# One of sixteen C products per tile, moved from VectorE to GpSimd, in a Mamba and mixture-of-experts kernel

## The chip, the cores and the metric

The kernel runs on one core of a Trainium2 chip. The metric is the device time of one execution, in microseconds (us). Below, PE is TensorE, DVE is VectorE, ACT is ScalarE, POOL is GpSimd and SP is SyncE, as in the profile; "span" is the stretch that the profiler covers, and times in timelines count from its start.

## What is computed

The reference is a selective state space layer and then a mixture of experts, on 4 sequences of 1024 tokens with 256 features. The change touches only the scan of the first layer and its product with C:

```python
deltaA  = jnp.exp(delta[..., None] * A)                 # (b, l, 512, 16)
deltaBx = (delta * xs)[..., None] * B[:, :, None, :]
_, ys = jax.lax.associative_scan(combine, (deltaA, deltaBx), axis=1)   # h = deltaA * h + deltaBx
y = jnp.einsum('blcn,bln->blc', ys, C)                  # sum over the 16 states
out = (y + xs * D) * res
return x + out @ w_out
```

All of it is float32. There are 512 channels and 16 states, so 8192 recurrences of 1024 steps for each sequence.

## The kernel before

**Tiles and steps.** The 4096 tokens are cut into 8 tiles (k = 0 to 7) of 512 tokens; a sequence is two tiles. A tile has 16 steps (q = 0 to 15, `NQ`), numbered Q = 16k + q over the run. A step handles 4 x 512 recurrence elements on each of 128 partitions, in four parts r = 0 to 3 (`NR`). The 16 steps are 4 channel chunks c of 4 steps f. After the eight tiles an expert stage follows, which the change does not touch.

**One step on the engines.**

- POOL, `input_step` (L474): one instruction of 128x2048 makes u times B into buffer `X[:, Q % 4]`; there are four buffers (`NX = 4`). It waits until the sum of step Q - 4 has been taken from that buffer (`y_acc`), and at the first step of a chunk until the replicated operand `rep` has arrived from memory.
- ACT, `decay` (L970): four exponentials of 128x512 into the four PSUM parts `psH[:, r]`. Each waits until the product of the step before has left that part (`hc_ready`). In even tiles `keep_state` (L959) first copies the last column of the part into `carry`, for the tile that continues the sequence.
- DVE, `scan` (L1135): four scans in place in `psH`, and `output_step` (L1144): four products `X = psH * C4`, each issued one scan later than the scan it reads. Step 9's last product is thus issued behind step 10's first scan.
- PE, `add_state` (L1492): four matmuls with `gsum` add the products to `psY`. They raise `y_acc` by one, which is what POOL waits for to reuse the buffer.

**The order of the rest.** All queues are written out by hand. PE's order for a tile is `PE_STEPS`: at step n it does the work `first`, then `add_state(Q - 1)`, then the work `rest`. Around the change these are:

```python
9:  ([("D", 0, 1)], [("D", 1, 1), ("R", 0, -1), ("R", 1, -1)]),
10: ([], [("L", 0, -1), ("U", 0, -1)]),
11: ([("U", 1, -1)], [("I", 4, 1)]),
12: ([("U", 2, -1)], [("N", 0, -1)]),
```

D is the projection of the next tile's time step (L1412), R the transposes of the previous tile's rows (L1419), L the router (L1429), U one part of the shared expert's first matrix (`up`, L1457), I the input projection (L1383), N the shared expert's second matrix (`down`, L1473). The router waits for ACT's two copies of the transposed rows (`read_nT`, recorded at the helper's line L800).

POOL's order after `input_step(k, q)`: at q = 4 and 6 `input_chunk(k, 2)` and `(k, 3)`, at q = 13 and 14 `input_chunk(k + 1, 0)` and `(k + 1, 1)` (four instructions of 128x512 each, L456 to L462, that make the operands which SP then stores and loads back as `rep`); at q = 3 `place`, at q = 4, 5, 6, 8 two scatters each, at q = 7 `roots`, at q = 15 `choose` (small instructions of the router of the tile before). SP loads the `rep` of the next tile's chunk 0 after `input_chunk(k + 1, 0)`, and that of chunk 1 (used from step 4) behind `load_c(k + 1, 3)`, which waits for step 15's last product.

Of the kernel before, what the change touches and what calls it, by code (L numbers as in the profile page):

```python
# [16 lines left out]
ALU = mybir.AluOpType  # L17
# [7 lines left out]
P = 128  # L25
TC = 512
# [21 lines left out]
def build(nc, x, norm_scale, w_in, conv_w, conv_b, A_log, D_skip, w_xproj, w_dt, b_dt, w_out,  # L48
# [4 lines left out]
    HALVES = L // TC  # L53
# [12 lines left out]
    NR = 4  # L66
    GJ = P // NR
    NF = N * GJ // P
    NG = N // NF
    NQ = CH * NF  # L70
# [38 lines left out]
    with ExitStack() as whole:  # L109
        def sem(name):  # L110
            return whole.enter_context(nc.semaphore(name))
# [52 lines left out]
        psH = whole.enter_context(nc.psum_tensor("psH", [P, NR, TC], F32))  # L164
# [11 lines left out]
        NX = 4  # L176
        X = big[:, half:].rearrange("p (n r t) -> p n r t", n=NX, r=NR)
# [34 lines left out]
        C4 = sb("C4", [P, NF, TC])  # L212
# [61 lines left out]
        scan_done = sem("scan_done")  # L274
        carry_done = sem("carry_done")
        hc_ready = sem("hc_ready")
        y_acc = sem("y_acc")
        z_done = sem("z_done")

# [111 lines left out]
                eng.wait_ge(p_free[bank_of(k, use)], PLACE[k, use] // 2 + 1)  # L391


        def products(Q, r):

            return Q * NR + r + 1

        def summed(Q):

# [28 lines left out]
        def _(pool):  # L428
# [35 lines left out]
            def input_step(k, q):  # L464

                c, f = q // NF, q % NF
                g, Q = k * CH + c, k * NQ + q
                if f == 0:
                    pool.wait_ge(rep_here[g % 2], 64 * (g // 2 + 1))
                if c == 0:  # L470
                    pool.wait_ge(b_here[f], 64 * (k + 1))
                if Q >= NX:
                    pool.wait_ge(y_acc, summed(Q - NX))
                nc.gpsimd.tensor_tensor(X[:, Q % NX], rep[:, g % 2, 1],  # L474
                                        B4[:, f:f + 1, :].broadcast_to([P, NR, TC]),
                                        ALU.mult).then_inc(bx_ready, 1)

            link = Chain(pool, p_link)

            def roots(k):  # L480
# [67 lines left out]
            for k in range(NT):  # L548
                for q in range(NQ):
                    input_step(k, q)  # L550
                    if q in (4, 6):
                        input_chunk(k, q // 2)
                    if k >= 2 and q == 3:
                        place(k - 2)
                    if k >= 2 and q in SCATTER_AT:
                        scatter(k - 2, SCATTER_AT[q])
                    if k >= 1 and q == 7:
                        roots(k - 1)
                    if k >= 1 and q == 15:
                        choose(k - 1)  # L560
                    if q in (13, 14) and k + 1 < NT:
                        input_chunk(k + 1, q - 13)
# [223 lines left out]
        def _(act):  # L786
# [168 lines left out]
            def keep_state(Q, r):  # L955
                k, q = Q // NQ, Q % NQ
                if Q >= 0 and k % HALVES == 0:
                    last = psH[:, r, TC - 1:TC]
                    nc.scalar.activation(carry[:, q, r:r + 1], last, ACT.Copy).then_inc(carry_done, 1)  # L959
                    act.wait_ge(carry_done, (k // HALVES) * NQ * NR + q * NR + r + 1)  # L960

# [123 lines left out]
        def _(dve):  # L1085
# [41 lines left out]
            def scan(k, q, r):  # L1127
                Q = k * NQ + q
                if r == 0:
                    dve.wait_ge(bx_ready, Q + 1)  # L1130
                    if k % HALVES:
                        dve.wait_ge(carry_done, (k // HALVES) * NQ * NR + (q + 1) * NR)
                dve.wait_ge(dA_ready, Q * NR + r + 1)
                start = carry[:, q, r:r + 1] if k % HALVES else 0.0
                nc.vector.tensor_tensor_scan(psH[:, r, :], psH[:, r, :], X[:, Q % NX, r, :], start,  # L1135
                                             ALU.mult, ALU.add).then_inc(scan_done, 1)

            def output_step(Q, r):

                f = Q % NF  # L1140
                if Q % NQ < NF:
                    dve.wait_ge(c_here[f], 64 * (Q // NQ + 1))
                dve.wait_ge(scan_done, Q * NR + r + 1)
                nc.vector.tensor_tensor(X[:, Q % NX, r, :], psH[:, r, :], C4[:, f, :],  # L1144
                                        ALU.mult).then_inc(hc_ready, 1)

# [211 lines left out]
        def _(pe):  # L1358
# [127 lines left out]
            def add_state(Q):  # L1486
                g, f = Q // NF, Q % NF
                if f == 0:
                    skip(g // CH, g % CH)
                for r in range(NR):  # L1490
                    pe.wait_ge(hc_ready, products(Q, r))
                    ins = nc.tensor.matmul(psY[r * GJ:(r + 1) * GJ, :], gsum[:], X[:, Q % NX, r, :],  # L1492
                                           start=False, stop=(f == NF - 1), skip_group_check=True)
                ins.then_inc(y_acc, 1)
# [26 lines left out]
            for k in range(NT + 2):  # L1521
                for n in range(NQ):
                    first, rest = pe_step(k, n)
                    Q = k * NQ + n
                    work(first)
                    if k < NT or (k == NT and n == 0):
                        if Q:
                            add_state(Q - 1)
                    work(rest)

# [80 lines left out]
```

## Time and profile before

| | |
|---|---|
| time, median of 3 runs | 1692.61 us (1691.77 to 1694.22) |
| the profiled execution: its own time | 1698.09 us |
| the profiled execution: span | 1696.1 us |
| scan stage (the eight tiles) | about 65 to 1055 us of the span |
| DVE busy over the span | 70% (in slices of the scan stage nine tenths or more) |
| POOL busy over the span | 56% |
| PE busy over the span | 87%, mean granted clock 0.925 |

Busy shares are averages over two stages with different limits. A row of a timeline gives start, duration, engine, line and operation, the shapes written and read, how many instructions are merged in it (x8), and in brackets the idle time before it with the engine that ended it. A matmul in float32 is recorded as two, so the four matmuls of `add_state` are x8.

### The profile page before, as it was taken

The page shows a single profiled execution, that of the slowest core. Times are in us where ns is not written, and L with a number is a line of the kernel's source. Part 1 is how long each engine was busy: PE and PEld are TensorE (multiplying, and loading weights), DVE is VectorE, ACT ScalarE, POOL GpSimd, SP SyncE. Part 2 cuts the span into 40 slices and gives each one's busy share as a digit, 9 for nine tenths or more (in the row PEclk, how much of TensorE's full clock was granted, in tenths as well). Part 3 has the DMA queues.
Part 4 walks back from the last instruction along what each step waited for, and adds up shares of the span by engine and source line. Part 5 has one row for each costly group of instructions (what it writes and reads, how often), then busy time and mean ns, then how long its engine had stood idle before and what let it go on. Part 6 is the DMA issues. An engine that isn't in the chain of part 4 may idle for free.

```text
span 1696.1 us, 24636 instructions
## 1 busy us (share of the span) xinstructions
PE 1474.3 (87%) x6945; PEld 958.2 (56%) x6946; DVE 1192.2 (70%) x2113; ACT 907.8 (54%) x1778; POOL 951.7 (56%) x590
## 2 busy tenths in 40 slices
PE   7386888999989989889989779989999999999970
PEld 3121324535535535436435335779999999999960
DVE  4489999999999999999999999213333333333327
ACT  4477667777766777766877543223233333323324
POOL 1586796898898898898898884301111111111115
PEclk9599997997998999998989789899999999999995
DMA  5833743663554545635635531745555555555538
GB/s 157 222 87 85 165 103 85 143 149 87 146 130 122 129 112 136 137 97 131 137 97 123 145 79 35 260 169 190 193 185 185 191 194 190 194 195 189 185 125 263
DMA packets 137447, 252.14 MB, mean 149 GB/s; under 512 B 15809, under 2 KB 68914, under 8 KB 137250
## 3 DMA queue, kind: packets, MB, share of 16 engines
q1 hardware_dynamic: 130898, 233.49, 49.8%
q0 software_dynamic: 6480, 17.83, 2.9%
q8 instruction: 30, 0.49, 0.1%
q14 instruction: 39, 0.32, 0.1%
HBM read 205.76 MB, written 45.51 MB: 148 GB/s over the span
## 4 chain that ended last, share of the span: by engine, by line
PE 45%; DVE 39%; issue 7%; ACT 6%; DMA 1%; SPq 1%; POOL 0%; DVEq 0%; ACTq 0%; POOLq 0%
DVE psH L1135 26%; PE psH L1553 15%; PE psP L1564 14%; DVE big L1144 8%; PE psP L1394 4%; PE psA L1492 2%; PE psA L1473 2%; PE psP L1457 2%; PE psP L1383 1%; PE psP L1503 1%; ACT psH L970 1%; PE psP L1541 1%; DVE res L1152 1%; ACT xs L846 1%; DVE st6f L1337 1%
## 5 line engine op out<-in xcount | busy, mean ns | idle before, releaser
L474 POOL TENSOR_TENSOR big<-big,B 128x2048 f32<-128x2048 f32 x128 | 578.2, 4531 | 103.1 <-PE psA L1492 46.2
L970 ACT ACTIVATE psH<-big,A_q 128x512 f32<-128x512 f32 x512 | 352.4, 691 | 155.1 <-DVE big L1144 129.3
L1144 DVE TENSOR_TENSOR big<-psH,C 128x512 f32<-128x512 f32 x512 | 345.3, 675 | 0.0
L1135 DVE TENSOR_TENSOR_SCAN psH<-psH,big 128x512 f32<-128x512 f32 x256 | 312.0, 1219 | 41.1 <-POOL big L474 20.9
L578 POOL DMA_INDIRECT con_dram<-eo,dest x71 | 68.1, 959 | 471.4 <-ACT eo L1043 463.5
L1135 DVE TENSOR_TENSOR_SCAN psH<-psH,carry,big 128x512 f32<-128x512 f32 x256 | 327.4, 1279 | 7.2 <-ACT psH L970 7.2
L1553 PEld LDWEIGHTS psH<-nTb,ew_s 128*128 128x128 f32 x2272 | 266.1, 193 | 4.2 <-issue 0.7
L1553 PE MATMUL psH<-nTb,ew_s 128*128 128x128 f32 x2272 | 266.5, 276 | 0.3 <-issue 0.3
L1564 PE MATMUL psP<-big,hT 128*128 x1136 | 257.0, 379 | 0.7 <-DVE eb L1302 0.7
L1492 PE MATMUL psA<-big,gsum 128*32 128x512 f32 x1024 | 224.1, 659 | 30.5 <-DVE big L1144 30.2
L1564 PEld LDWEIGHTS psP<-big,hT 128*128 128x128 f32 x1136 | 210.3, 190 | 26.8 <-issue 1.1
L1273 DVE TENSOR_TENSOR hT<-psH,vecs 128x512 f32<-128x512 f32 x142 | 98.2, 692 | 178.3 <-PE psH L1553 178.3
L1039 ACT ACTIVATE hT<-hT 128x512 f32<-128x512 f32 x142 | 89.4, 630 | 193.3 <-DVE hT L1273 192.2
L1383 PE MATMUL psP<-xnT,w_in_s 128*128 128x512 f32 x256 | 131.4, 639 | 29.8 <-ACT spr L800 26.8
L1457 PE MATMUL psP<-nT,sw_s 128*128 128x256 f32 x512 | 140.5, 427 | 0.5 <-ACT xs L800 0.5
L1457 PEld LDWEIGHTS psP<-nT,sw_s 128*128 128x128 f32 x512 | 108.2, 216 | 41.0 <-issue 18.2
L1394 PE MATMUL psP<-xraw,convd 128*128 128x512 f32 x256 | 120.2, 613 | 12.2 <-ACT xs L800 8.6
L1302 DVE TENSOR_TENSOR eb<-psP,eb_s 128x256 f32<-128x256 f32 x71 | 30.2, 425 | 141.0 <-PE psP L1564 141.0
L1492 PEld LDWEIGHTS psA<-big,gsum 128*32 128x32 f32 x1024 | 33.5, 111 | 167.5 <-DVE big L1144 117.0
L1473 PE MATMUL psA<-sw_s,hT 128*128 128x256 f32 x512 | 126.7, 395 | 0.0
L1043 ACT ACTIVATE eo<-eb,wt 128x256 f32<-128x256 f32 x71 | 36.1, 509 | 163.0 <-DVE eb L1302 163.0
L1473 PEld LDWEIGHTS psA<-sw_s,hT 128*128 128x128 f32 x512 | 98.0, 196 | 43.3 <-issue 30.6
(174 smaller groups left out, 1532.9 us busy)
## 6 DMA issues: line engine op xcount, KB each, us to landing
ew_s<-in_L_ffn_ew_dram SPq DMA_DIRECT2D x71, 1024.0 KB, 4.9
big<-ud_dram SPq DMA_DIRECT2D x128, 512.0 KB
ud_dram<-ud SPq DMA_DIRECT2D x32, 512.0 KB
xb<-rows_dram SPq DMA_DIRECT2D x71, 130.0 KB, 2.1
B<-bc_dram SPq DMA_DIRECT2D x128, 64.0 KB, 5.1
C<-bc_dram SPq DMA_DIRECT2D x128, 64.0 KB, 4.7
big<-in_L_ffn_ew_dram SPq DMA_DIRECT2D x8, 1024.0 KB
big<-con_dram SPq DMA_DIRECT2D x16, 512.0 KB, 8.8
```

Of the source, the lines that this page charges most:

```text
L474: nc.gpsimd.tensor_tensor(X[:, Q % NX], rep[:, g % 2, 1], B4[:, f:f + 1, :].broadcast_to([P, NR, TC]), ALU.mult).then_inc(bx_ready, 1)
L970: nc.scalar.activation(psH[:, r, :], rep[:, g % 2, 0, r, :], ACT.Exp, scale=A_q[:, c, r, f:f + 1]).then_inc(dA_ready, 1)
L1135: nc.vector.tensor_tensor_scan(psH[:, r, :], psH[:, r, :], X[:, Q % NX, r, :], start, ALU.mult, ALU.add).then_inc(scan_done, 1)
L1144: nc.vector.tensor_tensor(X[:, Q % NX, r, :], psH[:, r, :], C4[:, f, :], ALU.mult).then_inc(hc_ready, 1)
L1273: nc.vector.tensor_tensor(hT[:, par, a * (HC // 2):(a + 1) * (HC // 2), :], psH[:, 2 * par + a, :].rearrange("p (c t) -> p c t", t=P), bia ...
L1383: ins = nc.tensor.matmul(dst, w_in_s[:, d, m * P:(m + 1) * P], xnT[:, d, :], start=(d == 0), stop=(d == DC - 1))
L1394: ins = nc.tensor.matmul(dst, convd[:, j * CH + c, :], xraw[:, c % 2, j:j + TC], start=(j == 0), stop=(j == K - 1))
L1457: ins = nc.tensor.matmul(dst[:, j * 2 * P:(j + 1) * 2 * P], sw1_s[:, d, m * P:(m + 1) * P], nT[:, d, h * 2 * P:(h + 1) * 2 * P], start=(d ...
L1473: ins = nc.tensor.matmul(psS[:, t * O:(t + 1) * O], hT2[:, i % 2, j, t * P:(t + 1) * P], sw2_s[:, 2 * p + j, :], start=False, stop=(p == P ...
L1492: ins = nc.tensor.matmul(psY[r * GJ:(r + 1) * GJ, :], gsum[:], X[:, Q % NX, r, :], start=False, stop=(f == NF - 1), skip_group_check=True)
L1553: ins = nc.tensor.matmul(psH[:, 2 * par + a, j * P:(j + 1) * P], ew1_s[:, par, d, m * P:(m + 1) * P], nTb[:, par, d, :], start=(d == 0), s ...
L1564: ins = nc.tensor.matmul(psP[:, 1, 0:O], hT[:, par, m, :], ew2_s[:, e, m, :], start=(m == 0), stop=(m == HC - 1))
```

## The change

In step 9 of each tile (`QP = 9`, the tenth) DVE's four scans write into the buffer `X` instead of `psH` and raise `hc_ready` themselves; DVE makes no product for that step. POOL makes the product over the whole buffer in one instruction of 128x2048, in place. POOL does it after `input_step(k, 11)`, and waits for the four scans, for C, and in even tiles for ACT's four copies of the last column (which now read `X`). PE adds step 9 only when POOL's product is there (`by_pool`), and does so later in its order: not between R and L of step 10, but at n = 11 behind `first` (U1), just ahead of the sum of step 10.

```diff
+        QP = 9
+
         def products(Q, r):
 
-            return Q * NR + r + 1
+            swapped = {(QP - 1, NR - 1): 1, (QP, 0): -1}
+            return Q * NR + r + 1 + swapped.get((Q % NQ, r), 0)
+
+        def scanned(Q, r):
+
+            return Q * NR + r + 1 - NR * ((Q + NQ - 1 - QP) // NQ)
...
+            def output_step(k, q):
+
+                f, Q = q % NF, k * NQ + q
+                pool.wait_ge(hc_ready, products(Q, NR - 1))
+                pool.wait_ge(c_here[f], 64 * (k + 1))
+                if k % HALVES == 0:
+                    pool.wait_ge(carry_done, (k // HALVES) * NQ * NR + (q + 1) * NR)
+                nc.gpsimd.tensor_tensor(X[:, Q % NX], X[:, Q % NX], C4[:, f:f + 1, :].broadcast_to([P, NR, TC]),
+                                        ALU.mult).then_inc(by_pool, 1)
...
                     input_step(k, q)
+                    if q == QP + 2:
+                        output_step(k, QP)
...
-                    last = psH[:, r, TC - 1:TC]
+                    last = (X[:, Q % NX, r] if q == QP else psH[:, r])[:, TC - 1:TC]
...
-                nc.vector.tensor_tensor_scan(psH[:, r, :], psH[:, r, :], X[:, Q % NX, r, :], start,
-                                             ALU.mult, ALU.add).then_inc(scan_done, 1)
+                to = X[:, Q % NX, r, :] if q == QP else psH[:, r, :]
+                nc.vector.tensor_tensor_scan(to, psH[:, r, :], X[:, Q % NX, r, :], start,
+                                             ALU.mult, ALU.add).then_inc(hc_ready if q == QP else scan_done, 1)
...
+                if Q % NQ == QP:
+                    return
...
-                    pe.wait_ge(hc_ready, products(Q, r))
+                    if Q % NQ == QP:
+                        pe.wait_ge(by_pool, Q // NQ + 1)
+                    else:
+                        pe.wait_ge(hc_ready, products(Q, r))
...
-                        if Q:
+                        if Q and n != QP + 1:
+                            if n == QP + 2:
+                                add_state(Q - 2)
                             add_state(Q - 1)
```

## Rows read from the trace of the kernel before

**Rows 1.** The page, busy time of each engine over the span

```profile
PE 1474.3 (87%) x6945; PEld 958.2 (56%) x6946; DVE 1192.2 (70%) x2113; ACT 907.8 (54%) x1778; POOL 951.7 (56%) x590
```

**Rows 2.** The page, the costliest group of instructions by line

```profile
L474 POOL TENSOR_TENSOR big<-big,B 128x2048 f32<-128x2048 f32 x128 | 578.2, 4531 | 103.1 <-PE psA L1492 46.2
```

**Rows 3.** Timeline of VectorE, part of step 6, k = 4 (start, us, engine, line)

```profile
606.52 1.22 DVE L1135 TENSOR_TENSOR_SCAN psH<-psH,big 128x512 f32<-128x512 f32 x1
607.65 0.67 DVE L1144 TENSOR_TENSOR big<-psH,C 128x512 f32<-128x512 f32 x1
608.24 1.22 DVE L1135 TENSOR_TENSOR_SCAN psH<-psH,big 128x512 f32<-128x512 f32 x1
```

**Rows 4.** Timeline of GpSimd, k = 3, step 9 to the next tile's step 0

```profile
498.88 13.45 POOL L474 TENSOR_TENSOR big<-big,B 128x2048 f32<-128x2048 f32 x3
...
514.48 9.17 POOL L474 TENSOR_TENSOR big<-big,B 128x2048 f32<-128x2048 f32 x2 [2.15 <-PE psA L1492]
527.34 1.27 POOL L456 TENSOR_TENSOR spe<-spe,ud 128x512 f32<-128x512 f32 x1 [3.68 <-ACT ud L883]
...
532.51 4.53 POOL L474 TENSOR_TENSOR big<-big,B 128x2048 f32<-128x2048 f32 x1
...
542.17 4.54 POOL L474 TENSOR_TENSOR big<-big,B 128x2048 f32<-128x2048 f32 x1
...
549.87 4.54 POOL L474 TENSOR_TENSOR big<-big,B 128x2048 f32<-128x2048 f32 x1
```

**Rows 5.** Timeline of VectorE, k = 3, last scan of step 9

```profile
513.25 1.29 DVE L1135 TENSOR_TENSOR_SCAN psH<-psH,carry,big 128x512 f32<-128x512 f32 x1
```

**Rows 6.** Timeline of TensorE, k = 3, steps 9 to 11, and of ScalarE

```profile
517.40 1.63 PE L1492 MATMUL psA<-big,gsum 128*32 128x512 f32 x8
519.29 3.56 PE L1429 MATMUL psP<-rwT,nT 128*128 128x8 f32 x16 [0.25 <-ACT nT L800]
522.69 6.32 PE L1457 MATMUL psP<-nT,sw_s 128*128 128x256 f32 x16
528.95 1.06 PE L1492 MATMUL psA<-big,gsum 128*32 128x512 f32 x8
...
518.45 0.69 ACT L800 ACTIVATE nT<-psP,vecs 128x512 f32<-128x512 f32 x1
```

**Rows 7.** Timeline of TensorE, sum of step 10, k = 1, 4, 6; router, k = 4

```profile
283.18 1.06 PE L1492 MATMUL psA<-big,gsum 128*32 128x512 f32 x8
...
642.25 1.92 PE L1429 MATMUL psP<-rwT,nT 128*128 128x8 f32 x16 [0.76 <-ACT nT L800]
...
649.34 1.06 PE L1492 MATMUL psA<-big,gsum 128*32 128x512 f32 x8
...
898.03 1.07 PE L1492 MATMUL psA<-big,gsum 128*32 128x512 f32 x8
```

**Rows 8.** Timeline of VectorE, the first scan after k = 1, 3, 4, 6

```profile
313.11 1.22 DVE L1135 TENSOR_TENSOR_SCAN psH<-psH,big 128x512 f32<-128x512 f32 x1
...
559.68 1.22 DVE L1135 TENSOR_TENSOR_SCAN psH<-psH,big 128x512 f32<-128x512 f32 x1
...
681.41 1.28 DVE L1135 TENSOR_TENSOR_SCAN psH<-psH,carry,big 128x512 f32<-128x512 f32 x1
...
927.41 1.28 DVE L1135 TENSOR_TENSOR_SCAN psH<-psH,carry,big 128x512 f32<-128x512 f32 x1
```

**Rows 9.** Timeline of GpSimd, end of k = 0 and start of k = 1

```profile
164.80 4.51 POOL L474 TENSOR_TENSOR big<-big,B 128x2048 f32<-128x2048 f32 x1
...
179.82 9.01 POOL L474 TENSOR_TENSOR big<-big,B 128x2048 f32<-128x2048 f32 x2 [0.88 <-DMA big<-ud_dram]
```

**Rows 10.** Timeline of GpSimd, step 4 and step 8 in k = 4

```profile
576.16 4.54 POOL L474 TENSOR_TENSOR big<-big,B 128x2048 f32<-128x2048 f32 x1 [6.86 <-DMA big<-ud_dram]
...
615.58 4.52 POOL L474 TENSOR_TENSOR big<-big,B 128x2048 f32<-128x2048 f32 x1
```

**Rows 11.** Timeline of VectorE, k = 4, first scan of step 8

```profile
620.25 1.22 DVE L1135 TENSOR_TENSOR_SCAN psH<-psH,big 128x512 f32<-128x512 f32 x1
```

More of the change, by code:

```diff
@@ L276, in build @@
         hc_ready = sem("hc_ready")
+        by_pool = sem("by_pool")
         y_acc = sem("y_acc")
@@ L1134, in scan @@
                 start = carry[:, q, r:r + 1] if k % HALVES else 0.0
-                nc.vector.tensor_tensor_scan(psH[:, r, :], psH[:, r, :], X[:, Q % NX, r, :], start,
-                                             ALU.mult, ALU.add).then_inc(scan_done, 1)
+                to = X[:, Q % NX, r, :] if q == QP else psH[:, r, :]
+                nc.vector.tensor_tensor_scan(to, psH[:, r, :], X[:, Q % NX, r, :], start,
+                                             ALU.mult, ALU.add).then_inc(hc_ready if q == QP else scan_done, 1)
             def output_step(Q, r):
                 f = Q % NF
-                if Q % NQ < NF:
+                if Q % NQ == QP:
+                    return
+                if Q % NQ < NF or Q % NQ == QP + NF:
                     dve.wait_ge(c_here[f], 64 * (Q // NQ + 1))
-                dve.wait_ge(scan_done, Q * NR + r + 1)
+                dve.wait_ge(scan_done, scanned(Q, r))
                 nc.vector.tensor_tensor(X[:, Q % NX, r, :], psH[:, r, :], C4[:, f, :],
```

## The prediction, made before the changed kernel was run

> **What bounds the kernel now.** I first read the busy times on the page [rows 1]: PE is busiest over the span, but the change lies in the scan stage, where the slices of the page show DVE at nine tenths or more. So I went on to the timelines of that stage. They show a pair of scan and product on DVE starting every 1.72 us (606.52 to 608.24), the product taking 0.59 us of that: 607.65 to 608.24 [rows 3]. Four pairs are 6.9 us a step. Is DVE alone the bound? The second view is POOL's group for the products with B [rows 2]: 578.2 us in 128 instructions of 4.53 us, with 103.1 us idle ahead of them, most of it ended by PE's `add_state`. POOL is therefore held by buffers coming free as well as by its own work. In step 8 of tile 4 POOL's input ends at 615.58 + 4.52 = 620.10 [rows 10] and DVE's scan starts at 620.25 [rows 11]: there POOL has no lead at all. It has built up since step 4, whose input waits 6.86 us for the loaded `rep` [rows 10]. That load is released by the end of the previous tile's last product, so DVE's and POOL's ways through steps 0 to 8 both start at DVE's step 0. A delay or gain of that step passes on whole to the next tile. What counts is then how much earlier or later DVE can start step 0 of the next tile.
>
> **What DVE saves.** Four products leave step 9: 4 x 0.59 = 2.36 us a tile. The scans keep their shape, and only write elsewhere. A scan into SBUF has no row here; I take the 1.22 us of [rows 3], and would not expect the write alone to cost more than a few hundredths. A scan behind a scan has no row either. From below its distance is 1.13 us (606.52 to 607.65), which I take, since the parts are independent; from above it is the full 1.22 us, which would cost 4 x 0.09 = 0.36 us a tile. If nothing else held DVE, eight tiles would save 18.9 us.
>
> **What POOL's product costs.** It has the shape of the product with B: 4.53 us [rows 2]. In tile 3 POOL is through with the inputs of steps 9 to 11 at 498.88 + 13.45 = 512.33 [rows 4]. The last scan of step 9 ends at 513.25 + 1.29 = 514.54 [rows 5], less three removed products, 1.77, that stood ahead of it: 512.8. So POOL waits 0.5 us, makes the product to 517.3 and the input of step 12 to 521.9. DVE wants that input two steps after 512.8, at 526.6 or later, so nothing is late yet.
>
> The Trainium skill, "GPSIMD Engine Reference", section 4.1, speaks against such a move: elementwise work with two inputs belongs on VectorE, because GpSimd is about twice as slow. The rows say 4.53 against 2.36 us, so the trace agrees; by that rule alone 2.2 us of engine time would be lost a tile. Neither figure enters the sum, since the product fits into idle time.
>
> **What is late next.** The input of step 13 goes into the buffer of step 9, so it waits for `add_state` of step 9. Before, that sum ran at 517.40 to 519.03, in front of the router, which started at 519.29 behind ACT's copy (518.45 + 0.69 = 519.14) [rows 6]. It lay in time in which PE had to wait for ACT anyway. Now it is queued behind the router (3.56 us), U0 and U1 (6.32 us). The router can't start sooner, since ACT's copy ends when it did: it hangs on the D and R work before it. U1 therefore ends where the sum of step 10 started, at 528.95, and the sum of step 9 runs in its place, 1.06 us at the rate of that row, to 530.0 [rows 6]. POOL starts the input of step 13 some 0.15 us later (the input of step 12 started at 514.48), at 530.2. It has stood idle since 521.9.
>
> What is queued behind it on POOL: that input (4.53), the chunk for the next tile, the input of step 14, the other chunk, the input of step 15, `choose`, and the next tile's input 0. From the start of the chunk to the end of that input 0 the trace has 527.34 to 549.87 + 4.54 = 554.41, that is 27.07 us with no wait between [rows 4]. So the next tile's input 0 is ready 4.53 + 27.07 = 31.6 us after the input of step 13 starts, at 561.8. DVE's step 0 started at 559.68 [rows 8]. The result for tile 3: +2.1 us, where DVE by itself would have come 2.36 us early.
>
> **The same for the other tiles.** Ready = (end of step 10's sum) + 0.15 + 31.6, against DVE's old start. k = 1: 284.24 gives 316.0 against 313.11, +2.9. k = 4: 650.40 gives 682.15 against 681.41, +0.7. k = 6: 899.10 gives 930.85 against 927.41, +3.4 [rows 7, 8]. These are the first, the earliest and the last of the six tiles 1 to 6; tile 2 read the same way gives +3.5 and tile 5 +2.1. In even tiles POOL also waits for ACT's four copies. Each must come ahead of step 10's exponential of its part, so they are there when DVE is through with step 10 at the latest, and the 8 us of idle time before input 13 hold that too. Tile 0 has no shared-expert work on PE at this place and POOL has a lead, so it keeps -2.36; tile 7 prepares no next tile, -2.36.
>
> A second way leads over ACT: I4, U2 and N0 on PE come up to 1.06 us later, and with them ACT's reads and the exponentials queued behind them in step 13. That is under POOL's delay in all of the six but tile 4 (+0.7), where it could add 0.3 us at most. I leave it out.
>
> The sum: 2.9 + 3.5 + 2.1 + 0.7 + 2.1 + 3.4 - 2 x 2.36 = +10.0 us. The profiled execution took 1698.09 us by its own time, 2 us over its span, and would take 1708.1. It lies 5.5 us over the median of the runs shown, so for that median I predict 1692.6 + 10.0 = 1702.6 us.
>
> **The clock.** The same router took 3.56 us in tile 3 and 1.92 us in tile 4 [rows 6, 7]; the granted clock stood at half (1.2 GHz) in the one and at full (2.4 GHz) in the other. With step 9's sum gone from in front of the router, PE idles 1.6 us more there. If tile 4's router then falls to half clock too, its input 13 starts 1.64 us later. If the sum itself ran at the 1.63 us of [rows 6] instead of 1.06, six tiles would lose 3.4 us. I leave both out of the sum and in the range. From the other side, if the router ran at full clock in the five other tiles, the release would come 1.64 us sooner in each, 8.2 us in all: +1.8.
>
> The Trainium skill, "TensorE: Matmul & The Clock Gate", section "HAM oscillation — how this bites in real kernels", says that gaps in which PE is idle make the gate halve its clock. By that rule the wider gap ahead of the router can only cost; no row yet shows this gap.
>
> **The rivals.**
>
> - *The saving comes through (faster).* The place is the end of the chain above. If POOL's input 0 were ready by DVE's old start less 2.36 us, each tile would gain 2.36: 1692.6 - 18.9 = 1673.7 us. For that the input of step 13 would have to start 4.5 us sooner in tile 3, before 525.8. Then U1 would have to end 4.4 us sooner than 528.95, and PE's router and U0 and U1 (9.9 us together) would have to run at full clock throughout. Against it: only tile 4 comes near. Parts of it, with a net gain over 0.2%, are included: 0.11.
> - *No change.* The router's full clock of the paragraph above gives +1.8, 1694.4 us; likewise if half of the queue before U1 moved forward with DVE's earlier step 10. Against it: ACT's copy ends the router's wait, and it does not hang on step 9's products: 0.13.
> - *The loads come late (slower still).* The `rep` of the next tile's chunk 0 is stored and loaded after the first chunk. At the end of tile 0 the chunk ended at 164.80 and the load let POOL go at 179.82, 15.0 us later [rows 9]. In the chain above 17.4 us lie between (31.6 - 4.53 less the chunk's 5.17 and input 0's 4.54), so the load is hidden with 2.4 us to spare. If it takes 4.4 us longer, each of six tiles loses another 2 us: 1714.6. Chance 0.08.
> - *The forecast*, slower with POOL late: 0.68, with 1697 to 1709 us as its own range (the clock's 1.64 + 3.4 upward, half of its 8.2 and some more downward).
>
> The 0.2% that a measurement of this kernel can tell from no change is 3.4 us. The chances are then faster 0.11, same 0.13, slower 0.76. The range of 8 in 10 takes in the forecast and most of the case of no change: 1693 to 1710 us.
>
> **What would show it.** In the profile after: in step 9 DVE scans 1.1 to 1.2 us apart with no product; POOL's new line at 4.53 us, started within a microsecond or so of the last scan in odd tiles; then POOL idle some 8 us ahead of the input of step 13 in tile 3, ended by PE's `add_state`; that `add_state` directly behind U1; DVE waiting for POOL at step 15 and at step 0 of the next tile, in tiles 1 to 6. If POOL is idle there but DVE doesn't wait for it, my 31.6 us are wrong. If the sum of step 9 ends well before the old start of step 10's sum, PE's order is not the bound that I take it for, and the time comes out lower.

## The result: 0.9% slower, and the profile after

The changed kernel takes 1708.03 us (median of 4 runs, 1707.47 to 1708.63), the kernel before 1692.19 us beside it (1690.75 to 1694.22). The ratio is 1.0093, with a 95% interval of 1.0075 to 1.011: slower by 15.8 us. The profiled execution took 1707.71 us by its own time, with a span of 1705.9 us and a mean granted clock of 0.911. The page's busy times, and its chain of what ended last:

```profile
PE 1479.9 (87%) x6945; PEld 962.8 (56%) x6946; DVE 1175.7 (69%) x2081; ACT 905.8 (53%) x1778; POOL 987.1 (58%) x598
...
PE 45%; DVE 23%; POOL 15%; issue 8%; ACT 6%; DMA 1%; SPq 1%; DVEq 0%; POOLq 0%; ACTq 0%
```

Against [rows 1] DVE has 32 instructions and 16.5 us less, POOL 8 instructions and 35.4 us more. So the work moved as the diff says. In the chain POOL has 15%; in the chain of the kernel before it had 0%, and DVE 39%. The chain now runs over POOL. Its timeline in tile 3, to be held against [rows 4]:

```profile
502.38 13.48 POOL L482 TENSOR_TENSOR big<-big,B 128x2048 f32<-128x2048 f32 x3
517.67 4.52 POOL L493 TENSOR_TENSOR big<-big,C 128x2048 f32<-128x2048 f32 x1 [1.81 <-DVE big L1156]
522.15 4.53 POOL L482 TENSOR_TENSOR big<-big,B 128x2048 f32<-128x2048 f32 x1
534.37 4.55 POOL L482 TENSOR_TENSOR big<-big,B 128x2048 f32<-128x2048 f32 x1 [7.68 <-PE psA L1518]
...
561.39 13.49 POOL L482 TENSOR_TENSOR big<-big,B 128x2048 f32<-128x2048 f32 x3
```

L493 is the new product; L482 is the old L474, and L1518 the old `add_state`. The row at 534.37 is the input of step 13, the one at 561.39 begins with the next tile's input 0. POOL stands idle for 7.68 us before input 13, until PE has taken the sum of step 9. From there to input 0 POOL has no more waits. Why the sum comes late is in PE's timeline of the same place, beside [rows 6]:

```profile
521.08 0.66 PE L1442 MATMUL psP<-ident,xrow 128*128 128x128 f32 x4 [0.83 <-ACT spr L820]
523.54 3.55 PE L1452 MATMUL psP<-rwT,nT 128*128 128x8 f32 x16 [1.81 <-ACT nT L820]
526.95 6.32 PE L1480 MATMUL psP<-nT,sw_s 128*128 128x256 f32 x16
533.19 1.92 PE L1518 MATMUL psA<-big,gsum 128*32 128x512 f32 x16
```

The router (L1452) now starts 1.81 us after the transposes; U0 and U1 (L1480) follow, and the two sums (x16) come last. Who pays is DVE, at step 15 of this tile (558.26) and at step 0 of the next (565.94):

```profile
558.26 1.29 DVE L1156 TENSOR_TENSOR_SCAN psH<-psH,carry,big 128x512 f32<-128x512 f32 x1 [1.45 <-POOL big L482]
...
565.94 1.23 DVE L1156 TENSOR_TENSOR_SCAN psH<-psH,big 128x512 f32<-128x512 f32 x1 [0.48 <-POOL big L482]
```

**Where the time went.** The length of a tile is read here from its first scan (as in [rows 8]) to the next tile's, for tile 7 to the end of its last scan. In us, tiles 0 to 7:

| | 0 | 1 | 2 | 3 | 4 | 5 | 6 | 7 |
|---|---|---|---|---|---|---|---|---|
| before | 121.8 | 122.4 | 122.6 | 124.0 | 121.7 | 124.0 | 122.0 | 124.6 |
| after | 121.0 | 123.9 | 126.1 | 126.3 | 126.6 | 126.0 | 126.0 | 118.6 |
| after less before | -0.8 | +1.5 | +3.5 | +2.3 | +4.9 | +2.0 | +4.0 | -6.0 |
| predicted | -2.4 | +2.9 | +3.5 | +2.1 | +0.7 | +2.1 | +3.4 | -2.4 |

The eight add up to +11.4 us, against +9.8 for the spans. The one large miss on the losing side is tile 4. In the kernel before, its router and U ran at a granted clock of 0.76, in the changed kernel at 0.57 (columns: us, PE, PEld, DVE, ACT and POOL busy, PEclk, DMA share, GB/s). First the kernel before, from the router's start to U1's end in tile 4 and in tile 3:

```profile
642.20:649.40 7.20, 7.15 (x36) 6.02 (x40) 7.20 (x9) 7.07 (x15) 3.89 (x1) 0.76 0.19 67
519.20:529.00 9.80, 9.71 (x36) 8.29 (x40) 9.80 (x12) 7.95 (x13) 6.12 (x3) 0.55 0.14 40
```

The same two stretches of the changed kernel:

```profile
650.30:659.80 9.50, 9.48 (x36) 8.10 (x40) 8.78 (x15) 8.18 (x17) 7.74 (x2) 0.57 0.04 14
523.50:533.20 9.70, 9.66 (x34) 8.23 (x34) 9.65 (x17) 7.71 (x13) 3.19 (x1) 0.55 0.11 27
```

Tile 4's stretch grew from 7.2 to 9.5 us. Tile 3's was already long. The other 1.8 us by which tile 4's sum of step 9 came later than reckoned lie ahead of this stretch: the router started 84.4 us into the tile instead of 82.6. TensorE's clock was low there before the wider gap was reached, as the second half of the transposes shows, first in the kernel before, then in the changed one:

```profile
639.38 0.66 PE L1419 MATMUL psP<-ident,xrow 128*128 128x128 f32 x4 [0.82 <-ACT spr L800]
...
647.39 1.12 PE L1442 MATMUL psP<-ident,xrow 128*128 128x128 f32 x4 [0.37 <-ACT spr L820]
```

### The profile page after: what moved, and what is told of

Its sections match the earlier page's. It is cut to its first block, busy times and chain, and to the rows that moved or that the text cites. A ratio compares the mean times of both kernels' runs of the same rounds, so it can differ in the third digit from the quotient of the medians.

```text
span 1705.9 us, 24652 instructions
## 1 busy us (share of the span) xinstructions
PE 1479.9 (87%) x6945; PEld 962.8 (56%) x6946; DVE 1175.7 (69%) x2081; ACT 905.8 (53%) x1778; POOL 987.1 (58%) x598
## 4 chain that ended last, share of the span: by engine, by line
PE 45%; DVE 23%; POOL 15%; issue 8%; ACT 6%; DMA 1%; SPq 1%; DVEq 0%; POOLq 0%; ACTq 0%
PE psH L1581 15%; PE psP L1592 14%; DVE psH L1156 14%; POOL big L482 9%; PE psP L1417 4%; DVE big L1167 4%; PE psA L1518 2%; PE psP L1406 2%; PE psA L1496 2%; PE psP L1480 1%; PE psP L1435 1%; POOL big L493 1%; ACT psH L990 1%; POOL ud L467 1%; POOL ud L470 1%
## 5 line engine op out<-in xcount | busy, mean ns | idle before, releaser
L482 POOL TENSOR_TENSOR big<-big,B 128x2048 f32<-128x2048 f32 x128 | 578.2, 4533 | 65.7 <-PE psA L1518 39.6
L990 ACT ACTIVATE psH<-big,A_q 128x512 f32<-128x512 f32 x512 | 352.0, 690 | 149.6 <-DVE big L1167 125.9
L1156 DVE TENSOR_TENSOR_SCAN psH<-psH,big 128x512 f32<-128x512 f32 x240 | 292.0, 1219 | 61.1 <-POOL big L482 30.8
L1167 DVE TENSOR_TENSOR big<-psH,C 128x512 f32<-128x512 f32 x480 | 322.8, 673 | 0.0
L1156 DVE TENSOR_TENSOR_SCAN psH<-psH,carry,big 128x512 f32<-128x512 f32 x240 | 306.3, 1278 | 19.2 <-ACT psH L990 12.5
L1518 PE MATMUL psA<-big,gsum 128*32 128x512 f32 x1024 | 212.5, 652 | 43.0 <-DVE big L1167 35.0
L1406 PE MATMUL psP<-xnT,w_in_s 128*128 128x512 f32 x256 | 144.0, 692 | 29.3 <-ACT spr L820 26.9
L1480 PE MATMUL psP<-nT,sw_s 128*128 128x256 f32 x512 | 140.0, 426 | 0.5 <-ACT xs L820 0.5
L1518 PEld LDWEIGHTS psA<-big,gsum 128*32 128x32 f32 x1024 | 31.5, 112 | 179.1 <-DVE big L1167 115.6
L1480 PEld LDWEIGHTS psP<-nT,sw_s 128*128 128x128 f32 x512 | 107.5, 215 | 41.0 <-issue 17.7
```

The costliest lines, as they stand in the source:

```text
L482: nc.gpsimd.tensor_tensor(X[:, Q % NX], rep[:, g % 2, 1], B4[:, f:f + 1, :].broadcast_to([P, NR, TC]), ALU.mult).then_inc(bx_ready, 1)
L990: nc.scalar.activation(psH[:, r, :], rep[:, g % 2, 0, r, :], ACT.Exp, scale=A_q[:, c, r, f:f + 1]).then_inc(dA_ready, 1)
L1156: nc.vector.tensor_tensor_scan(to, psH[:, r, :], X[:, Q % NX, r, :], start, ALU.mult, ALU.add).then_inc(hc_ready if q == QP else scan_done, 1)
L1406: ins = nc.tensor.matmul(dst, w_in_s[:, d, m * P:(m + 1) * P], xnT[:, d, :], start=(d == 0), stop=(d == DC - 1))
L1480: ins = nc.tensor.matmul(dst[:, j * 2 * P:(j + 1) * 2 * P], sw1_s[:, d, m * P:(m + 1) * P], nT[:, d, h * 2 * P:(h + 1) * 2 * P], start=(d ...
```

## The experiments

Each is timed in rounds beside the kernel before on the same chip, save `before_again`, which is one profiled execution. The theory is the prediction's: the place of the sum in PE's order holds POOL's buffer. The rivals are POOL's product itself, and the clock.

**The order alone.** On the kernel before: DVE still makes all products.

```diff
-                        if Q:
+                        if Q and n != 10:
+                            if n == 11:
+                                add_state(Q - 2)
                             add_state(Q - 1)
```

> The kernel before with one edit: DVE still makes all products, but PE adds step 9 where the changed kernel does, at n = 11 behind U1 and ahead of the sum of step 10. Theory (the place of the sum in PE's order holds the buffer of step 9 and with it POOL): POOL's input 13 starts at the same moment as in the changed kernel, 94 to 95 us into a tile, and the next tile's step 0 is as late; the product on DVE lies in time in which DVE waits for POOL anyway. So the time is near that of the changed kernel, 1703 to 1710 us. Rival (GpSimd's additional 4.53 us of work a tile is what makes it late): the time stays near the kernel before, 1690 to 1694 us.

Measured: 1712.54 us against 1693.17, ratio 1.0103 (1.0086 to 1.012). POOL in tile 3 of this kernel, inputs 12 and 13:

```profile
521.94 4.53 POOL L474 TENSOR_TENSOR big<-big,B 128x2048 f32<-128x2048 f32 x1 [3.12 <-PE psA L1492]
...
537.68 4.54 POOL L474 TENSOR_TENSOR big<-big,B 128x2048 f32<-128x2048 f32 x1 [11.21 <-PE psA L1492]
```

The whole loss of the changed kernel is there without any product on POOL: it comes from moving one sum behind U1. The time is 2.5 us over the range expected. By tiles this kernel is 1.2, 1.6 and 2.4 us longer than the changed one in tiles 0, 1 and 7 (122.2, 125.5 and 121.0 us) and within 0.4 in the five between; so DVE's saving is seen in tiles 1 and 7, perhaps in tile 0, and nowhere else.

**The sum one place earlier.** On the changed kernel, with the sum of step 9 between U0 and U1:

```diff
+                    if k < NT and n == QP + 2:
+                        add_state(Q - 2)
                     work(first)
...
-                            if n == QP + 2:
-                                add_state(Q - 2)
```

> The changed kernel with PE's sum of step 9 one place earlier, ahead of U1. Theory: the sum ends about 2.5 us sooner in each of tiles 1 to 6 (half of the 6.3 us that U0 and U1 take, less a slower sum), so input 13 and the next tile's step 0 come that much sooner: 1708 - 15 = 1693 us, 1689 to 1698. Rival (GpSimd's added work): POOL's order is untouched, so no change from 1708 us.

Measured: 1689.40 us, ratio 0.9968 (0.9951 to 0.9985). One part of U less in front of the sum turns a loss of 0.9% into a gain of 0.3%. It ends 90.2 to 91.8 us into the tile here, 92.2 to 94.9 in the changed kernel.

**Earlier still.** Between the router and U0:

```diff
-                    work(rest)
+                    if k < NT and n == QP + 1:
+                        work(rest[:1])
+                        add_state(Q - 1)
+                        work(rest[1:])
+                    else:
+                        work(rest)
```

> The changed kernel with PE's sum of step 9 between the router and U0. Theory: the sum ends some 5.5 us sooner than in the changed kernel; POOL's input 0 is then ready before DVE wants it in odd tiles, and about level in even tiles, where POOL's product waits for ACT's copies of the state until 82 to 83 us into the tile. What is left of the 2.36 us a tile on DVE shows: 1675 to 1690 us, 1683 expected, with PE 1.6 us later at U0 and U1. Rival (GpSimd's added work): 1708 us.

Measured: 1692.76 us, ratio 0.9994 (0.9984 to 1.0004). A miss: the sum now ends at 86.1 to 88.4 us, POOL is no longer late, and still nothing is gained over the version with the sum ahead of U1. Against that version DVE's waits for POOL fell over the span from 25.2 us in 9 to 21.1 in 2, and its waits for PE's output projection, which the residual needs, rose from 5.8 us in 2 to 12.0 in 8 (3.19 us of it in tile 7). The waits for ACT's exponentials, 37.8 us in 30, were there already (37.5 in 30; 27.4 in 16 in the kernel before).

**The old place.** In front of the router, on the changed kernel:

```diff
-                        if Q and n != QP + 1:
-                            if n == QP + 2:
-                                add_state(Q - 2)
+                        if Q:
                             add_state(Q - 1)
```

> The changed kernel with PE's sum of step 9 where the kernel before has it, ahead of the router. Theory: in odd tiles GpSimd's product ends at 81 to 82.5 us into the tile, when PE comes to the sum, so the old course is back. In even tiles the product ends at 87 us, and the router and all of PE's work behind it start 3 to 4 us later, which ACT and DVE then wait for. Between the kernel before and the one above: 1680 to 1697 us, 1689 expected. Rival (GpSimd's added work): 1708 us or more.

Measured: 1706.41 us, ratio 1.0073 (1.0056 to 1.0089). A miss, 9 us over the range. PE in tile 4:

```profile
649.39 1.93 PE L1518 MATMUL psA<-big,gsum 128*32 128x512 f32 x8 [5.54 <-POOL big L493]
```

In tiles 2, 4 and 6 PE stands 5.1 to 5.5 us in front of this sum, and the router behind it, since POOL's product isn't there. So the sum can't simply stay where it was; why the product is late follows below.

**The kernel before once more.**

> The kernel before, unchanged, for a second profile. The first profiled execution took 1698.1 us, 5.5 over its median, with 36.2 us for steps 0 to 3 of tile 7 where tiles 3 and 5 took 32.6. If that was a single late stretch, this one lacks it and the span is 1690 to 1694 us; the difference to the changed kernel's span is then near 15 us instead of 9.8.

Measured: a span of 1694.4 us, its own time 1696.42 us, clock 0.933. The tiles took 120.9, 122.4, 121.6, 124.0, 121.7, 124.0, 122.0 and 124.6 us; only tiles 0 and 2 differ from the first profile, by about 1 us each. The guess was wrong: the long stretch in tile 7 is there again, and the span is above the range. But the clock differs in tile 1. Its router and the two parts of U behind it, in the first profile and in this one:

```profile
273.51 3.56 PE L1429 MATMUL psP<-rwT,nT 128*128 128x8 f32 x16 [0.26 <-ACT nT L800]
...
272.06 1.92 PE L1429 MATMUL psP<-rwT,nT 128*128 128x8 f32 x16 [0.46 <-ACT nT L800]
273.84 5.39 PE L1457 MATMUL psP<-nT,sw_s 128*128 128x256 f32 x16
```

The sum of step 10 began 92.5 us into the tile in the one and 88.7 in the other, and the tile took 122.4 us both times. In the kernel before, nothing waits there for that work.

**A quarter of POOL's product.** On the changed kernel:

```diff
-                nc.gpsimd.tensor_tensor(X[:, Q % NX], X[:, Q % NX], C4[:, f:f + 1, :].broadcast_to([P, NR, TC]),
+                nc.gpsimd.tensor_tensor(X[:, Q % NX, 0, :], X[:, Q % NX, 0, :], C4[:, f, :],
```

> The changed kernel with GpSimd's product over one of the four parts of step 9 only (128x512 instead of 128x2048; three parts stay unmultiplied), so some 1.3 us instead of 4.53. Theory (place of the sum): the product lies in time in which GpSimd waits for the sum, so in tiles 1 to 6 nothing moves: 1708 us, 1705 to 1710. Rival (GpSimd's added work counts): 3.3 us less in each of eight tiles, 1682 us.

Measured: 1707.70 us (1707.41 to 1708.86), ratio 1.0078 (1.0061 to 1.0095); the changed kernel has 1708.03. POOL is 25 us less busy (962.1 against 987.1), and no time is gained: the product lies in idle time.

**Step 10 instead of 9.** `QP = 10`, which puts the sum of step 10 behind U2.

> The changed kernel with QP = 10: the eleventh step is treated so instead of the tenth, and everything that hangs on it moves by one step. Theory: now the input of step 14 waits for the late sum, which comes behind U2 at about 99 us into a tile. It stands behind input 13 and a chunk on GpSimd, which end at about the same time, so the next tile's input 0 comes only 2 to 3 us later than in the kernel before, which had 3 to 5 us of lead. The saving on VectorE shows in every tile: 1692 - 8 x 2.36 = 1673 us, 1671 to 1684 with losses where the lead was 3 us. Rival (GpSimd's added work): about 1708 us as for step 9.

Measured: 1705.76 us, ratio 1.0064 (1.0047 to 1.0081). A miss. Tiles 2, 4 and 6 take 125.0, 126.9 and 126.8 us, but tiles 1, 3 and 5 only 121.0, 124.0 and 122.0. POOL in tile 4:

```profile
653.30 4.55 POOL L493 TENSOR_TENSOR big<-big,C 128x2048 f32<-128x2048 f32 x1 [8.57 <-ACT carry L979]
```

and ACT's last copy of the carry there:

```profile
652.94 0.19 ACT L979 ACTIVATE carry<-big 128x1 f32<-128x1 f32 x1
```

In the even tiles 0, 2, 4 and 6 the product waits not for DVE's scans but for four copies of 0.2 us, each of which stands in ACT's order ahead of the next step's exponential of its part. In the changed kernel it is the same wait. POOL's product there, by its line:

```profile
  ACT carry L979: 29.2, 4
  DVE big L1156: 11.0, 3
```

29.2 us in four waits for the copies, 11.0 in three for the scans. In tiles 2, 4 and 6 (5.5 to 5.8 us each) nothing hangs on it, since POOL waits another 2.9 to 3.4 us ahead of input 13. In tile 0 (12.5 us) POOL's queue has no further wait up to input 15, so there the wait counts.

**The copies earlier.** To test that reading: as the last, but in even tiles ACT makes the copies of parts 1 to 3 together, ahead of the second exponential of step 11 (and wait there for the last of step 10's four scans).

```diff
+                early = q == QP + 1 and k % HALVES == 0
...
+                if not early or r == 0:
+                    keep_state(Q - 1, r)
+                elif r == 1:
+                    for other in range(1, NR):
+                        keep_state(Q - 1, other)
```

> The kernel with QP = 10, and in even tiles ScalarE makes its copies of the state of parts 1 to 3 of step 10 one after the other ahead of step 11's second exponential, instead of one ahead of each. In the run without this, GpSimd's product started 5 to 6.5 us after VectorE's last scan of step 10 in even tiles and the next tile's input 0 ended at 125 to 127 us. Theory (the product waits for ScalarE's copies, which stand behind reads of TensorE's results): the product now starts within 1 us of the scan in even tiles too, about 84.5 us into the tile, input 0 ends near 121.5 us, and three even tiles gain 3 to 5 us each: 1706 - 12 = 1694 us, 1689 to 1699. Rival (TensorE's late sum of step 10 sets it): no change from 1706 us.

Measured: 1684.16 us against 1695.36, ratio 0.9938 (0.9919 to 0.9957). The product of tiles 2, 4 and 6 now starts 85.7, 87.6 and 85.1 us into the tile, in the run before 88.9, 90.8 and 90.7. Moving three copies is worth about 1.25%, some 21 us, more than the 7 to 17 expected. 12 of them are in these three tiles (121.8, 123.8 and 121.2 us), 2.2 in tile 0, which is even too. The rest is in the odd tiles; that it comes from POOL being less late there wasn't tested.

**Step 8 instead.** `QP = 8`. The place ahead of the sum of step 9 at n = 10 is in front of the router.

> The changed kernel with QP = 8. Theory: the late sum then stands ahead of step 9's sum and of the router, about 82 us into a tile. Input 12 starts 4 us later than before, input 13 at 86.5, and GpSimd still comes to the next tile's first chunk at 91 to 92 us, when ScalarE has its operands ready as before. So no delay at the tile's end, and VectorE gains; but one of the four removed products lay in a stall for ScalarE's exponentials in step 8, so 1.8 us a tile: 1692 - 14 = 1678 us, 1673 to 1685. Rival (GpSimd's added work): about 1708 us.

Measured: 1679.65 us (1678.39 to 1681.41) against 1695.2, ratio 0.9916 (0.99 to 0.9933). PE in tile 3:

```profile
510.35 2.76 PE L1518 MATMUL psA<-big,gsum 128*32 128x512 f32 x16
513.04 1.95 PE L1452 MATMUL psP<-rwT,nT 128*128 128x8 f32 x16
514.85 3.70 PE L1480 MATMUL psP<-nT,sw_s 128*128 128x256 f32 x16
```

Both sums stand ahead of the router, with no gap before it, and the clock is full from there on:

```profile
513.00:518.50 5.50, 5.50 (x40) 4.77 (x36) 5.50 (x7) 4.62 (x9) 5.50 (x2) 1.00 0.03 12
```

This is the fastest version found. Its six middle tiles take 119.9 to 122.2 us.

**Two steps, 0 and 8.** `QPS = (0, 8)`, the counts of the waits widened to match, the sum of step 0 placed behind what is no U at n = 1, POOL's product of it after input 3.

> Two steps a tile are treated so, 0 and 8; step 0's product follows input 3 on GpSimd, in time in which GpSimd waits for the loaded operand of step 4, and TensorE adds step 0 ahead of the last part of its work at n = 1. If that idle time holds the product and the sum comes before 16.5 us into the tile, VectorE saves 2.36 us more in each tile: 1680 - 19 = 1661 us. In even tiles ScalarE's copies let the product start at 10 to 11 us only and the sum ends near 17, so input 4 comes 1 us late and, with no lead left at step 8, so does that step: 1660 to 1680 us, 1670 expected. If GpSimd's total work has become the bound, 1680 us or more.

Measured: 1684.53 us, ratio 0.9939 (0.992 to 0.9958). A miss: by the ratios it is 0.23% slower than step 8 alone. The two intervals overlap, but its fastest run (1683.66 us) is slower than the slowest of step 8's. Tiles 3 and 5 take 125.6 and 125.9 us. DVE's wait there:

```profile
448.33 0.69 DVE L1189 SCALAR_TENSOR_TENSOR xrow<-xrow,psP 128x512 f32<-128x512 f32 x1 [5.71 <-PE psP L1533]
```

PE waited 2.69 us for the product at n = 1; the output projection behind it came late, and DVE's residual with it (35.0 us in 9 waits, against 3.8 in one with step 8 alone).

**The gap filled.** The runs so far don't separate PE's order from PE's clock. This one keeps the changed kernel's order and adds three matmuls of 128x512 in the gap between R and the router, in tiles 1 to 7. Nothing reads what they write.

```diff
+                    if 1 <= k < NT and n == QP + 1:
+                        pe.wait_ge(rwT_ready, 1)
+                        after(pe, acc_done, 4 * (k - 1))
+                        for i in range(3):
+                            nc.tensor.matmul(psS, skipd[:, 0, :], xs[:, k % 2, 0, :], start=True, stop=True,
+                                             skip_group_check=True)
                     work(rest)
```

> The changed kernel with three extra float32 matmuls (128x512 each, into psS, whose value they destroy for nobody: the next use starts it anew) on TensorE between the transposes R and the router, where the kernel before has the sum of step 9 and the changed one waits 1.8 us for ScalarE. Theory (that gap keeps the granted clock at its lower level through router and U0, U1, which in tile 4 makes the late sum later still): in the even tiles that were partly at full clock before (4 and 6, and by the second profile of before also 2) the late sum ends 2 to 4 us sooner, near 90.7 to 93 us into the tile: 1708 - 8 = 1700 us, 1697 to 1704. Rival (the clock falls for what lies ahead of it, the 3.8 us wait for the projection, and the gap has no part in it): the late sum stays at 94 to 95 us in all six tiles, 1706 to 1710 us.

Measured: 1693.73 us against 1694.33, ratio 0.9995 (0.9981 to 1.0008). That is 14 us faster than the changed kernel, with more work, and below the range expected. PE in tile 3:

```profile
519.59 4.44 PE L1561 MATMUL psA<-xs,skipd 128*128 128x512 f32 x6
523.86 1.85 PE L1452 MATMUL psP<-rwT,nT 128*128 128x8 f32 x16
525.56 3.70 PE L1480 MATMUL psP<-nT,sw_s 128*128 128x256 f32 x16
529.19 1.92 PE L1518 MATMUL psA<-big,gsum 128*32 128x512 f32 x16
```

and the granted clock from the router on, in tiles 4 and 3:

```profile
646.80:652.20 5.40, 5.40 (x34) 4.64 (x32) 4.54 (x6) 4.01 (x9) 5.40 (x2) 1.00 0.00 0
523.80:529.20 5.40, 5.40 (x35) 4.65 (x33) 4.76 (x6) 3.46 (x7) 0.93 (x1) 1.00 0.18 49
```

Router, U0 and U1 take 5.4 instead of 9.7 us, at full clock instead of 0.55. Tiles 1 to 6 take 122.9, 123.7, 124.2, 122.7, 123.0 and 122.7 us: all six are shorter, the odd ones too. (Tile 0, which the edit doesn't touch, took 122.3 against 121.0, so a single tile can move by a microsecond or so.) The extra matmuls don't fit into the pause: in tile 3 the router starts 85.9 us into the tile instead of 83.9. Nor did they keep the clock from falling: while they ran (519.6 to 523.8) the granted clock was 0.59, and from the router on it was full.

**The same matmuls in the kernel before**, as a check that a faster clock isn't worth the same anywhere.

> A control for the run before it: the kernel before, with the same three extra matmuls between the sum of step 9 and the router. If the extra matmuls took 14 us off the changed kernel because its own gap ahead of the router kept the clock low, the kernel before, which has the sum of step 9 there and no such gap, gains little: VectorE waits only a few us a tile for ScalarE in steps 10 to 13, and the matmuls themselves take 1.6 to 3 us of TensorE's time: 1688 to 1698 us. Rival (they are worth as much anywhere): near 1680 us.

Measured: 1696.98 us against 1694.22, ratio 1.0011 (1.0001 to 1.0021). PE in tile 3:

```profile
521.80 3.07 PE L1533 MATMUL psA<-xs,skipd 128*128 128x512 f32 x6
524.71 1.85 PE L1429 MATMUL psP<-rwT,nT 128*128 128x8 f32 x16
526.42 3.70 PE L1457 MATMUL psP<-nT,sw_s 128*128 128x256 f32 x16
```

The router and U speed up here as well, from 9.7 to 5.4 us in all, and there is no gain in all: with the sum of step 9 ahead of them, no buffer waits for their end. By tiles it isn't even: tile 7 took 121.0 us instead of 124.6, tile 2 took 124.1 instead of 122.6 or 121.6.

## Why the prediction was right, and where its sum was off

**DVE's saving: right.** Three of the four scans of step 9 in tile 3, of the changed kernel:

```profile
511.80 1.27 DVE L1156 TENSOR_TENSOR_SCAN big<-psH,carry,big 128x512 f32<-128x512 f32 x1
...
513.58 2.44 DVE L1156 TENSOR_TENSOR_SCAN big<-psH,carry,big 128x512 f32<-128x512 f32 x2
```

Two scans back to back take 2.44 us, so the second starts 2.44 - 1.27 = 1.17 us after the first, between the two bounds given (1.13 and 1.22). Writing to SBUF costs nothing that shows: 1.27 us, where the same kind of scan into PSUM had a mean of 1.28. DVE's busy time fell by 16.5 us where 8 x 2.36 = 18.9 were reckoned.

**POOL's product in idle time: right.** It takes 4.52 us and starts 1.81 us after input 11's end, where 0.5 was reckoned, and `quarter_product` shows its length to be free. In even tiles ACT's copies held it up by 5.5 to 5.8 us, and POOL's idle time ahead of input 13 held that too, in tiles 2, 4 and 6. The rule that the prediction weighed, of the Trainium skill, "GPSIMD Engine Reference", section 4.1 (GpSimd about twice as slow for such work), has its ratio right, 4.52 against 2.36 us. Those microseconds were not on the path.

**The sum of step 9 behind U1: right, and shown to be the cause.** In tile 3 it was to end at 530.0 on the clock of the old trace, 94.3 us into a tile that began at 435.7; it ended at 94.6. The order alone does it without POOL's product (1712.5 us), and one place earlier it is gone (1689.4 us). The chain over POOL's queue to the next tile's step 0 held as well: DVE waits for POOL at step 15 of tiles 1 to 6 and at the step 0 behind tile 1 to tile 6, and from tile 3's input 13 to the next input 0's end POOL took 561.39 + 4.5 - 534.37 = 31.5 us, where 31.6 were reckoned. The way over ACT, left out of the sum, shows as well: between 190 and 1052 us of the span DVE waited for ACT's exponentials 32.7 us in 24 waits, against 17.3 in 10 before. Since the last wait of each of the six tiles is for POOL, POOL set their length.

**The clock: the term that was mis-sized.** The prediction saw that the gap ahead of the router would widen by 1.6 us. It called 1.64 us in tile 4 possible and left it out, so that tile 4 got +0.7; it took +4.9. Its sum of step 9 ended 4.1 us later than reckoned: the router grew from 1.92 to 3.55 us and U from 5.39 to 6.08, and the router started 1.8 us later, with the clock low in D and R already.

For the other tiles the prediction took the low clock over from the trace of before, and that this came out right was luck. The second profile of the same kernel had its router at full clock in tiles 1 and 2 as well. Read in the same way, (end of step 10's sum) + 31.75 less DVE's start, it gives -0.9, +0.8, +2.0, +0.8, +2.1 and +3.4 us for tiles 1 to 6. Less the 4.72 us saved in tiles 0 and 7, that is +3.4 us instead of +10.0, just the 3.4 us that the prediction took as the bound of "no change". In the changed kernel all six routers took 3.5 us or more.

In saying that the order costs 10 us, the prediction took for a price of the order what is a price of order and slow clock together: with the gap filled, the changed kernel stands at -0.05% (-0.19 to +0.08%) against the one before. The rival "no change" had named the condition, the router at full clock, and a time of 1694.4 us; the run in which the condition was brought about has 1693.73. That the two are so close is chance in part, since the rival reckoned 1.64 us a tile for the router alone, while in the run U sped up too and the router started later. What wasn't seen is that the kernel's own order, what PE has to do just before the router, goes with that clock: low in all six tiles of the changed kernel, of `order_alone` and of `quarter_product`, full in all six of `gap_filled`.

The Trainium skill, "TensorE: Matmul & The Clock Gate", section "HAM oscillation — how this bites in real kernels", says that idle gaps make the gate halve the clock and that the work after them then starts slow. By that rule the router should run slow behind the wider gap, and `gap_filled` should undo it; the trace agrees in the outcome (tile 3: 0.55 with the gap, 1.00 filled). That the gap is what makes the clock fall isn't shown. The Trainium skill's example there is a longer wait, for a DMA. Tile 3 of the kernel before had 0.55 with a gap of only 0.25 us, in tile 4 of the changed kernel the clock was low ahead of the gap, and in `gap_filled` it was low while the extra matmuls ran and came back only then. No run here settles what lets it fall.

**Tiles 0 and 7.** The two gained 0.8 and 6.0 us where 2.36 each were forecast. In tile 7, steps 0 to 3 took 36.2 us before and 32.6 after, and these 3.6 aren't the saving: DVE's residual stood waiting there for PE's output projection in the kernel before,

```profile
951.92 0.69 DVE L1162 SCALAR_TENSOR_TENSOR xrow<-xrow,psP 128x512 f32<-128x512 f32 x1 [3.48 <-PE psP L1503]
```

and has no wait in the changed one. The wait is gone too in `order_alone` and in `before_filled`, where DVE makes all products and tile 7 took 121.0 us. The remaining 2.4 are the saving. In tile 0 DVE was 2.4 us ahead at step 14 (105.7 us into the tile against 108.1) and only 0.9 at step 15 (114.1 against 115.0), where it waited 1.47 us for POOL. POOL had no lead left, since its product had stood 12.5 us for ACT's copies; the prediction had held tile 0 safe. Against the second profile of before (107.1 and 114.0) nothing of the saving is left in tile 0.

**The base.** The tiles' misses cancel, tile 4's +4.2 against tile 7's -3.6 and tile 0's +1.6 against tile 1's -1.4. Against the profiled execution the prediction had 1708.1 us, and the profiled execution of the changed kernel took 1707.71; that they agree so closely is luck. The 5.4 us by which the median was missed are the 5.5 us taken off at the end, on the assumption that the changed kernel's median would lie as far under its profile as that of before did. It didn't: 1708.03 against 1707.71. Eight of the eleven timed experiments lay within 1.5 us of their profile too. Why the first profile of before lay so high is open; its second was 1.2 us over the median beside it (1696.42 against 1695.2).

**What stays open.** How much of the 14 us is the router's and U's clock in each tile can't be told from the medians alone, since the extra matmuls also move the router's start, by 0.2 us (tile 4) to 3.1 us (tile 1). What lets the clock fall isn't known, nor why tile 7 of the kernel before waits for the output projection.

## What to carry to other kernels

When an instruction that releases a buffer is moved behind others in a written-out order, cost the release and not the instruction: add up what now stands in front of it at the clock that this stretch will have, and follow the released engine's whole queue to the next place where someone waits. Before moving work off a busy engine, choose the step by what follows it in the other queues: the same move changed the time by +0.9% at step 9, +0.6% at step 10 and -0.8% at step 8. Read TensorE's granted clock around a stretch that something waits for, in more than one profile: ten microseconds of work at half speed became 5.4 when three matmuls were put in front of it. That matters only if somebody waits for their end.

## What the hardware showed that was not expected

- Three matmuls that nobody needs, put in where TensorE had paused for 1.81 us, shortened the router and U from 9.7 to 5.4 us, and the kernel by 14 us (1708.03 to 1693.73). In the kernel before the same three shortened them as much and were worth nothing.
- A product in place over 128x2048 on GpSimd takes 4.52 us, as long as one into another buffer (4.53), beside scans on VectorE that take 1.27 us (1.28 in the kernel before).
